# First attention layer of a four-layer graph network: the own-row product on GpSimd, and own part plus sum joined on VectorE for two of the four heads

## What is computed

```python
xl = (h @ Wg_l + bg_l).reshape(n, heads, d)
...
alpha = a / denom[d2]
out = jax.ops.segment_sum(alpha[:, :, None] * xl[s2], d2, num_segments=n)
out = out.mean(axis=1) + b_gat
mu = out.mean(-1, keepdims=True)
var = out.var(-1, keepdims=True)
out = (out - mu) * jax.lax.rsqrt(var + 1e-05) * gamma + beta
return jax.nn.elu(out)
```

## Time and profile before

| what | value |
|---|---|
| median of 3 runs | 9756.26 us (9750.86 to 9763.2) |
| the profiled execution's own time | 9752.56 us |
| its span, first to last instruction | 9750.8 us |
| mean granted TensorE clock over the span | 0.798 |
| PE / DVE / ACT / POOL busy over the span | 61% / 58% / 33% / 67% |
| the first attention stage (L2511 from 7347.6 us, last L2532 at 7952.5 us) | about 605 us |

### The profile page before, as it was taken

The page is one execution under the profiler, slowest core; times in us unless marked ns, Lnnn a source line. Parts: engine busy times, 40 slices in busy tenths (PEclk is TensorE's granted clock), DMA queues, the critical chain, the costliest instruction groups (busy, mean ns, idle before and its releaser), DMA issues. The chain is left out here.

```text
span 9750.8 us, 81928 instructions
## 1 busy us (share of the span) xinstructions
PE 5932.8 (61%) x20315; PEld 3138.0 (32%) x20315; DVE 5680.1 (58%) x17056; ACT 3198.3 (33%) x5481; POOL 6491.2 (67%) x6270
## 2 busy tenths in 40 slices
PE   6556666666669856555555200898877976600487
PEld 6523232233335422222222100343224544300254
DVE  4246665665656566666666688444448865510676
ACT  0034333333423333333333111443435653300244
POOL 6667777777777577777777777775740017767466
PEclk7578888887889977778777555999998988855799
DMA  5843322222269722222223222222324532222353
GB/s 143 111 145 112 103 97 97 88 97 89 96 174 261 213 90 92 93 92 95 91 91 94 79 80 74 70 74 58 72 52 151 164 120 73 72 48 52 96 156 118
DMA packets 1070263, 1018.15 MB, mean 104 GB/s; under 512 B 637543, under 2 KB 693237, under 8 KB 1057241
## 3 DMA queue, kind: packets, MB, share of 16 engines
q1 hardware_dynamic: 797158, 880.41, 28.6%
q0 software_dynamic: 200352, 130.16, 6.8%
q10 hardware_dynamic: 72275, 2.32, 1.0%
HBM read 492.47 MB, written 597.21 MB: 112 GB/s over the span
## 5 line engine op out<-in xcount | busy, mean ns | idle before, releaser
L732 POOL DMA_INDIRECT gathered<-u,place_of_source x1564 | 1655.6, 1059 | 528.5 <-issue 475.9
L732 POOL DMA_INDIRECT gathered<-hop,place_of_source x1564 | 1622.2, 1037 | 525.8 <-issue 475.7
L786 DVE SCALAR_TENSOR_TENSOR first_node_sum<-sums,ends_first,first_node_sum 128x64 f32<-128x64 f32 x4290 | 1191.1, 278 | 7.9 <-DVE sums L776 7.2
L762 DVE TENSOR_TENSOR weighted<-gathered,bank 128x512 f32<-128x512 f32 (+1 forms) x490 | 335.2, 684 | 1242.3 <-DMA gathered<-hop,place_of_source 569.3
L776 DVE SCALAR_TENSOR_TENSOR sums<-sums,same_as_before,weighted 128x64 f32<-128x64 f32 x3510 | 971.2, 277 | 62.0 <-DVE weighted L762 40.2
L732 POOL DMA_INDIRECT gathered<-x,row_of_source x782 | 810.7, 1037 | 293.1 <-issue 233.5
L2483 POOL DMA_INDIRECT out_dram<-lane_out,node_to_write x392 | 386.9, 987 | 272.7 <-ACT lane_out L2402 166.6
L501 PE MATMUL bank<-dense_tmp,mean 128*128 128x512 f32 x980 | 523.0, 651 | 44.4 <-ACT dense_tmp L510 42.9
L732 POOL DMA_INDIRECT pair<-h_sage,row_of_source x391 | 403.8, 1033 | 209.9 <-issue 123.4
L732 POOL DMA_INDIRECT gathered<-y,place_of_source x391 | 409.7, 1048 | 192.3 <-issue 118.9
L732 POOL DMA_INDIRECT gathered<-in_x_dram,dst_index x392 | 396.8, 1012 | 180.3 <-issue 118.0
(11 more groups left out here) (510 smaller groups left out, 15058.2 us busy)
## 6 DMA issues: line engine op xcount, KB each, us to landing
head_sums<-head_sums SPq DMA_DIRECT2D x98, 1024.0 KB, 4.7
y<-conv_out SPq DMA_DIRECT2D x294, 256.0 KB
conv_out<-y SPq DMA_DIRECT2D x245, 256.0 KB, 3.1
hop<-sums SPq DMA_DIRECT2D x196, 256.0 KB
turned<-rows_turned SPq DMA_DIRECT2D x196, 256.0 KB, 2.6
cat<-turned SPq DMA_DIRECT2D x196, 256.0 KB, 5.1
u<-conv_out SPq DMA_DIRECT2D x196, 256.0 KB
lane_raw<-x SPq DMA_DIRECT2D x196, 256.0 KB
```

Of the source, the lines that this page charges most:

```text
L732: return e.indirect_dma_start(out=into, out_offset=None, in_=tab, in_offset=bass.IndirectOffsetOnAxis(ap=index, axis=0), bounds_check=top, ...
L762: e.tensor_tensor(weighted[g % 2][:, 0:n, :], st.rows_of(g), over(st.weight[:, cols], D), ALU.mult).then_inc(st.weighed.handle, 1)
L786: e.scalar_tensor_tensor(h, row_, flast[:, t:t + 1], h, ALU.mult, ALU.add).then_inc(st.headed.handle, 1)
```

## The change

With `v2`, the product of own rows and own shares moves from VectorE to GpSimd, in a loop of its own over the 49 groups, with the same five buffers and the same count `owned`. `first_heads` comes after that loop. VectorE instead adds `head_sums` to `heads` for the first 128 of each 256 columns (two of four heads), 128x8x128 values per group, in place in `heads`, and counts the new semaphore `joined`. TensorE waits for `joined` too and leaves out the second transposing matmul for these heads (c equal to 0), so 24 are left of 32. In the second attention layer nothing is changed.

```diff
@@ -2297,6 +2297,7 @@
+        joined = sem("weighed", NG if v2 else 0)
@@ -2346,8 +2347,10 @@
-                            e.matmul(to, o[:, at_], ident[:], start=True, stop=False, is_transpose=True)
-                            m = e.matmul(to, s[:, at_], ident[:], start=False, stop=True, is_transpose=True)
+                            alone = v2 and c == 0
+                            m = e.matmul(to, o[:, at_], ident[:], start=True, stop=alone, is_transpose=True)
+                            if not alone:
+                                m = e.matmul(to, s[:, at_], ident[:], start=False, stop=True, is_transpose=True)
@@ -2374,6 +2377,8 @@
                     e.wait_ge(*(fixed(1) if g == NG - 1 else summed((g + 1) * K8 - 1)))
+                    if v2:
+                        e.wait_ge(*joined(g + 1))
@@ -2471,11 +2476,18 @@
-                    for g in range(NG):
+                    for g in range(NG if v2 else 0):
+                        l = g % LANES
+                        if g >= 5:
+                            e.wait_ge(*turned_in(g - 5))
+                        e.wait_ge(*mine_in[l](16 * (g // LANES + 1)))
+                        e.tensor_tensor(heads_of(O[g % 5][:]), each_head(mine[l], K8), per_head(shares(g)[:, HEADS:, :], K8),
+                                        ALU.mult).then_inc(owned.handle, 1)
+                    if v2:
+                        first_heads()
+                    for g in range(0 if v2 else NG):
                         if g == NG - 4:
                             first_heads()
-                        if v2:
-                            continue
@@ -2526,17 +2538,22 @@
                         steps.to(due(g, 0.6))
-                        if g >= 5:
-                            e.wait_ge(*turned_in(g - 5))
-                        e.wait_ge(*(mine_in[l](16 * (g // LANES + 1)) if v2 else lanes[l].loaded[0](16 * (g // LANES + 1))))
-                        e.tensor_tensor(heads_of(o[:]), each_head(mine[l], K8), per_head(shares(g)[:, HEADS:, :], K8),
-                                        ALU.mult).then_inc(owned.handle, 1)
+                        if not v2:
+                            if g >= 5:
+                                e.wait_ge(*turned_in(g - 5))
+                            e.wait_ge(*lanes[l].loaded[0](16 * (g // LANES + 1)))
+                            e.tensor_tensor(heads_of(o[:]), each_head(mine[l], K8), per_head(shares(g)[:, HEADS:, :], K8),
+                                            ALU.mult).then_inc(owned.handle, 1)
                         steps.to(due(g, 0.8))
@@
+                        if v2:
+                            e.wait_ge(*owned(g + 1))
+                            e.wait_ge(*summed(c0 + n - 1))
+                            e.tensor_tensor(o[:, :, 0:P], o[:, :, 0:P], s[:, :, 0:P], ALU.add).then_inc(joined.handle, 1)
                         steps.to(due(g, 1))
```

## The result

The changed kernel takes 9800.15 us (median of 5 runs, 9793.12 to 9806.69), the kernel before 9756.26 (9745.67 to 9763.2): a ratio of 1.0045, 95% interval 1.0032 to 1.0058. It is slower by 44 us, 0.45%. The forecast had the direction, slower by 134 us, and was three times too large.

What follows compares the result with a forecast made beforehand. TensorE with ScalarE's short answers was taken to bound the stage at 12.63 us a group; 15.4 us instead, 2.8 more times 48, added 134 us to 9752.56, giving 9887, as median 9890, range 9728 to 9960.

Steps and rivals of the forecast that it cites:

- What bounds the stage: Mid-stage, TensorE with ScalarE's short answers sets the 12.63 us group period; VectorE works 11.34 us and waits 1.29.
- The transposes: On TensorE, eight transposes fewer per group save 0.87 us, taking its round from 12.63 to 11.76 us.
- no-cost rival: GpSimd's product costs VectorE nothing: groups take 11.8 to 12.2 us, -20 to -42 us, about 9726; chance 0.17.
- VectorE's own work: Per group on VectorE: 11.34 us less 2.29 for the product plus 1.21 for the addition, 10.26 us.
- The stop: VectorE's two-input SBUF work stands still for GpSimd's whole product, 4.7 us a group; chance 0.62, range 9820 to 9960.
- GpSimd's product: The multiplication of 2,048 elements on GpSimd, 49 times, bounded between 1.9 and 4.7 us and taken as 4.7.
- the ring: Path through VectorE and TensorE, L553 via step 16 and `center` to next L553: 11.2 to 12.2 us, 15.9 to 16.9 if stopped.
- partial-cost rival: VectorE loses half of GpSimd's time, 2.35 us, or the product is shorter: period 13.5, +42 us, about 9800; chance 0.14.
- The clock: TensorE's granted clock falls as its busy share drops to about 69%: +25 to +50 us more, 9915 to 9940; chance 0.05.

Runs made afterwards that it cites:

- write-only run: Changed kernel, but GpSimd fills `heads` with a constant instead of multiplying, reading nothing; 9728.79 us, ratio 0.9958 to the kernel before.
- The copy: Changed kernel, but GpSimd copies own rows into `heads` four times over, one input tile, instead of multiplying; 9741.03 us, ratio 0.997 to the kernel before.
- own-rows-first: Changed kernel, but SyncE issues the load of own rows ahead of the store of sums and the features load; 9913.72 us, ratio 1.0143 to the kernel before.
- the run with the product twice: Changed kernel, but GpSimd makes each product twice, first into a spare tile nobody reads; 9972.35 us, ratio 1.0207 to the kernel before.

## Why the prediction was right in its direction and wrong in its size

**What bounds the stage.** Right: TensorE's round set the pace, VectorE had 1.29 us to spare. The product alone on GpSimd used up about this reserve and cost nothing that can be told.

**The transposes.** Right: TensorE's round without VectorE in its way was forecast at 11.76 us and is 11.76 in the write-only run. The no-cost rival had -20 to -42 us; the write-only run has -46, as L519's lateness at `center` mostly vanished in the waits behind it (TensorE waits 2.2 us there in 34 groups).

**VectorE's own work.** 10.26 us forecast, 10.08 measured. The addition takes 1,218 ns (1.21 forecast), but the next instruction starts 1.13 us after its start.

**The stop.** The mechanism was right, and it was a choice between two bounds that no row of before decided. The Trainium skill's rule in SBUF — State Buffer, "Who interferes with whom", is met in each part that the runs touch: two SBUF inputs on VectorE's side, a reading GpSimd instruction on the other, nearly the whole instruction (3.31 us of 3.75), either one waiting for the other.

**The step that failed** is the size put on the stop: "With the stop, VectorE alone needs 10.26 + 4.7 = 14.96 us a group", and with it "I take 15.4". The terms, with what they measured:

| term | forecast | measured |
|---|---|---|
| GpSimd's product | 4.7 us | 3.75 |
| of it, time in which VectorE stands | all | 3.31 |
| VectorE's own work | 10.26 us | 10.08 |
| period with the stop among the sums | 14.96 | 13.39 |
| added for a stop in the ring | 0.44 | 0 |
| first L553 to last L553 | 48 x 2.8 = 134 us more | 31.7 us more |
| first multiplication to first L553 | not counted | 9.9 us more |

The last two rows are 639.3 us against 607.6, and 37.7 against 27.8. With the end of the stage, which is 0.7 us shorter, they make the 40.9 us. Period by period the forecast is 15.4 - 13.39 = 2.0 us too long: 0.95 from the product's size, 0.44 from counting all of it as stop, 0.44 from the ring and 0.18 from VectorE's own work.

The largest part is the product's size. I had taken the select on 128 elements with its fixed cost spread over every element, 2.3 ns each; the product needs 1.8. The two rows of numbering had shown a fixed part of 0.12 us. With that taken off, the select's rate is 1.3 ns, and the product would have come out at 2.9 us, which is as much too short as 4.7 was too long. So the rows gave two bounds, and the end of the range was taken for the value. The 4,497 ns of the Trainium skill (GPSIMD Engine Reference, "Performance versus the Vector engine"), stated for an addition, is also longer than this product's 3.75 us. Second, a product's record is 0.4 us longer than what it takes from VectorE (twice: 6.65 us for two of 3.7 and 3.9).

**The ring** was sized right but did not apply to the changed kernel. I let the product start 5.2 us behind the sums, by a landing time of 4.4 us. The load took 5.7, and the product started 6.7 us behind the sums (7605.9 to 7612.65), 0.8 us into the next ones. The load is now issued right behind that of the features, which may be why it takes longer; no run separates this. Two experiments put the stop ahead of step 16 with the clock at 1.00. The copy's period of 13.30 us less its 1.57, and the own-rows-first period of 14.38 less 3.51 - 0.74 = 2.77, leave a ring of 11.7 and 11.6 us, inside the forecast's 11.2 to 12.2. That the own-rows-first run averages 15.5 us a group, close to the 15.4 forecast, is luck: its stop is shorter than the 4.7 us assumed, and a slower clock made up for it.

**The partial-cost rival** (0.14) named about 9800 us, which is what came, but not the way it came. It had a stop of 2.35 us inside the ring; the stop is 3.31 us and lies among the sums. The no-cost rival's remark that above a stop of 0.4 to 0.8 us the kernel is slower also holds for the ring only: among the sums the copy's 1.66 us left the kernel 34 us faster.

**Not counted:** the stage's start, where three products run in a row. It was in the text of the kernel (three loads are issued ahead), and the rule that GpSimd "runs about two groups ahead" had led me to take it as harmless.

**The clock** stayed at 1.00 in the changed kernel with TensorE busy 77%, so this rival (0.05) did not come there. It did in two experiments: at 0.87 in the run with the product twice, where VectorE set the pace and it cost nothing that shows, and at 0.91 with own rows first, where TensorE is in the ring and it cost about half of the 95 us.

## What to carry to other kernels

Before moving elementwise work from VectorE to GpSimd, count it on both sides: while GpSimd reads SBUF, VectorE instructions with two SBUF inputs stand still, so a 2.3 us product that became a 3.7 us product elsewhere still cost VectorE 3.3 us. What ran beside them here without a stop is a GpSimd instruction that only writes, and VectorE work with one input in PSUM. Then ask where the stop falls: the copy's stop of 1.6 us cost 1.5 us a group on the path that runs through both engines and nothing where VectorE had that much to spare. When two engines are as close as here (11.34 and 12.63 us a group), look for a part of the change that shifts only as much work as the reserve holds, as the addition for six of eight tiles does. And where rows only bound a duration, as 2.9 and 4.7 us did here, work the sum out at both ends.

## What the runs showed of the hardware

GpSimd's product of 2,048 f32 values per partition, with both inputs broadcast, takes 3.68 to 3.77 us in the steady part of the changed kernel, a one-input copy 1.90, a fill 1.81. GpSimd waits for VectorE in its turn: its product took 4.48 us behind an addition under way. A wait of this kind shows in the trace as a longer instruction, not as idle time: one sum of 485 ns became one of some 3.8 us. Stops add up: two products in a row held up a single run of sums for 6.65 us, and three at the start for 9.9 us. Where TensorE waited for VectorE in the own-rows-first run, its granted clock went to 0.50 for some 6 us, and `center` took 2.07 us instead of 1.02.
